# GpSimd divides the attention probabilities by their sums in place, ahead of the transposes

## The chip, the cores and the metric

One core of one Trainium2 chip runs the whole kernel. The metric is device time in microseconds (us), the median of several executions. Engines: TensorE (PE; PEld is its weight load), VectorE (DVE), ScalarE (ACT), GpSimd (POOL) and SyncE (SP), which only issues transfers.

## What is computed

One transformer block with adaptive layernorm over x of shape (8, 512, 256) in float32: latent attention with 16 heads and a causal mask, then a mixture of 16 experts (top 4, capacity 128) with a shared expert. The part that the change touches is the softmax and what follows it:

```python
scores = jnp.einsum('bqhd,bkhd->bhqk', q_full, k_full) * scale
scores = jnp.where(causal[None, None], scores, -1e30)
probs = jax.nn.softmax(scores, axis=-1)
attn = jnp.einsum('bhqk,bkhd->bqhd', probs, v)
return attn.reshape(b, s, NH * DV) @ w_o
```

The kernel applies the key and value projections on the query and output side, so that `kmat` (the latent keys, 64 columns, and the rotary part) serves as keys and values of all heads.

## The kernel before, in words

The outer loop runs over the 8 batches (512 rows each, 4 tiles of 128), the inner one over 8 pairs of heads. The order of the instructions on each engine is written out by hand, and semaphores connect the engines. `step` exists for TensorE, ScalarE and VectorE and does one pair p (g = 8b + p counts pairs); `middle` does what lies between two batches: the attention output, second layernorm, shared expert and routing of batch b, and the projection of batch b + 1. The last pair of a batch (`last`) also carries the first layernorm of the next batch, where the other pairs carry the next pair's queries.

A pair has 8 units: for each of its two heads the four query tiles from last to first, 512, 384, 256 and 128 keys wide (`UNITS`, `UW`). For each unit:

- TensorE forms the scores in PSUM (L650 to L652, three passes).
- VectorE adds the mask, takes the negated maximum and writes the shifted scores to `probs` in SBUF (`maxima`, L1231).
- ScalarE takes the exponential in place and leaves the row sums in `psums` (`exps`, L987).
- TensorE transposes `probs` in blocks of 128 x 128 to PSUM, in six groups (`GROUPS`, `turn_probs`, L671); ScalarE copies groups 0, 1, 2 and 4 to `pT` (L996), VectorE groups 3 and 5 (L1248).
- TensorE multiplies `pT` with the values in `kmat` (`values`, L692), during the next pair's step.

The sums take a way of their own. VectorE inverts the 8 sums (L1237) and widens them to 128 x 512 (`wide`, L1238); TensorE transposes that in four blocks (`spread_sums`, L681) to PSUM bank 4; ScalarE copies it to `rb` (`sums_out`, L1004); and VectorE multiplies the result of `values` by it (`values_out`, L1257).

The order on TensorE in a step is: next pair's query projection in two halves with the scores of units 3 to 7 between, `values` of the pair before, `turn_probs` groups 0 and 1, `q_turn` (L636, the next queries, which wait for VectorE's rotary steps L1210 to L1224), groups 2 and 3, groups 4 and 5, `spread_sums`, and the next pair's scores of units 0 to 2. Unit 0 of the next pair writes bank 0, where group 3 was, so it waits for VectorE's copy of group 3:

```python
pe.wait_ge(*((pT_dve, 2 * g - 1), (pT_act, 4 * g), (pT_act, 4 * g - 1))[u])
```

On VectorE the step is: maxima of units 3 and 4, then 5 to 7, the rotary steps for the next queries, `invert_sums`, `values_out`, `q_low` (L1262, which waits for ScalarE's copy of the turned queries, L982), the copies of groups 3 and 5, `q_low` again, maxima 0 to 2. In the last pair of a batch `h1_statistics` (L1178, L1181) stands behind the maximum of unit 4 and `h1_normed` (L1185) in the place of the rotary steps; TensorE then turns h1 (L762) in two parts in the place of `q_turn`, ScalarE copies each part, and the second part waits for the copy of the first.

GpSimd has its own loop over the batches: the roots for the first layernorm (`root`, L471 and L473, two operations, which wait for `var1_ready`), roots for the rms norms, `post` (roots of the second layernorm, its scale and shift, a copy of x), `counts` (the routing counts, behind `mask_ready`), `shared`, and `scatter`, 16 indirect DMAs, three to a pair, each three held until that pair's `values` are done.

## Time and profile before

| | us |
|---|---|
| median of 3 runs | 1249.4 |
| lowest, highest | 1245.29, 1251.21 |
| the profiled execution, its own time | 1254.99 |
| its span, first to last instruction | 1253.1 |
| TensorE busy | 1177.9 |
| VectorE busy | 836.0 |
| ScalarE busy | 667.2 |
| GpSimd busy | 276.5 |

Busy time is the time in which an engine has an instruction in work. TensorE's matmuls overlap one another, and their ends are modelled, so distances between starts say more than durations. The granted TensorE clock was 0.978 of full speed over the span, and 1.00 in the stretches from 570 to 740 us that are read below. Times within the trace count from the span's start.

### The profile page before, as it was taken

The numbers are of one execution on the slowest core, as the hardware profiler recorded it, in microseconds if no ns is written. First come the engines' busy times: TensorE is split into PE (matmuls) and PEld (weight loads), VectorE is DVE, ScalarE is ACT, GpSimd is POOL, SyncE is SP. The second block draws the span as 40 slices with busy tenths as digits, with TensorE's granted clock in tenths as the row PEclk, the third lists the DMA queues.
The fourth block names the chain that finished last, engine by engine and source line by source line (L and its number), as shares of the span: only waits on it lengthen the run. The fifth ranks groups of instructions, "written<-read, shape, count | busy, mean of one in ns | idle before, by whom it ended". The sixth has DMA issues, their size and how long they took to land.

```text
span 1253.1 us, 26074 instructions
## 1 busy us (share of the span) xinstructions
PE 1177.9 (94%) x7620; PEld 953.2 (76%) x7620; DVE 836.0 (67%) x2581; ACT 667.2 (53%) x1920; POOL 276.5 (22%) x332
## 2 busy tenths in 40 slices
PE   6799999999999999999999999999999999996782
PEld 3688778887888778887888778877888778873441
DVE  3677568776777667775877677766877577756221
ACT  2476626663567536763576447663667356731220
POOL 1000122211221122113212131212221122102553
PEclk9999999999999999999999999999999999997977
DMA  9410001000200001000100001000100010004752
GB/s 304 142 57 0 1 18 51 0 0 0 67 0 0 0 17 50 0 0 11 56 0 0 0 17 50 0 0 17 50 0 0 0 50 1 0 1 136 210 129 38
DMA packets 48317, 46.17 MB, mean 37 GB/s; under 512 B 10048, under 2 KB 44960, under 8 KB 48296
## 3 DMA queue, kind: packets, MB, share of 16 engines
q1 hardware_dynamic: 29096, 30.90, 8.1%
q0 software_dynamic: 7168, 6.37, 2.8%
q10 hardware_dynamic: 12032, 8.65, 2.4%
q8 instruction: 10, 0.16, 0.1%
q14 instruction: 11, 0.09, 0.0%
HBM read 35.04 MB, written 15.11 MB: 40 GB/s over the span
## 4 chain that ended last, share of the span: by engine, by line
PE 84%; DMA 5%; DVE 4%; issue 2%; ACT 2%; SPq 1%; POOL 1%; POOLq 0%; DVEq 0%; ACTq 0%
PE PS L671 11%; PE PS L692 10%; PE PS L802 8%; PE PS L650 7%; PE PS L651 6%; PE PS L652 6%; DMA out<-x_res,toku 5%; PE PS L636 4%; PE PS L810 4%; PE PS L831 3%; PE PS L623 3%; PE PS L626 2%; PE PS L627 2%; PE PS L624 2%; PE PS L625 2%; PE PS L781 2%
## 5 line engine op out<-in xcount | busy, mean ns | idle before, releaser
L987 ACT ACTIVATE probs<-probs,nmax 128x512 f32<-128x512 f32 (+3 forms) x512 | 283.0, 554 | 124.5 <-DVE nmax L1231 121.5
L1231 DVE CUSTOM_DVE_ANT_0 probs<-PS,cmask 128x512 f32<-128x512 f32 (+3 forms) x512 | 229.3, 488 | 98.6 <-PE PS L652 96.2
L540 POOL DMA_INDIRECT tab_dram<-entry,slot x112 | 110.5, 986 | 392.4 <-PE PS L692 371.1
L650 PE MATMUL PS<-kTh,qTh 128*128 128x512 f32 (+3 forms) x512 | 177.5, 347 | 1.7 <-DVE qTl L1262 1.5
L651 PE MATMUL PS<-kTl,qTh 128*128 128x512 f32 (+3 forms) x512 | 164.9, 322 | 0.0
L652 PE MATMUL PS<-kTh,qTl 128*128 128x512 f32 (+3 forms) x512 | 164.9, 322 | 0.0
L996 ACT ACTIVATE pT<-PS 128x384 f32<-128x384 f32 (+3 forms) x320 | 127.3, 462 | 70.6 <-PE PS L671 70.5
L671 PE MATMUL PS<-ident,probs 128*128 128x128 f32 x1280 | 164.8, 275 | 0.0
L692 PE MATMUL PS<-pT,kmat 128*64 128x512 f32 (+3 forms) x1024 | 151.9, 439 | 0.3 <-issue 0.3
L671 PEld LDWEIGHTS PS<-ident,probs 128*128 128x128 f32 x1280 | 141.4, 140 | 10.3 <-issue 7.4
L692 PEld LDWEIGHTS PS<-pT,kmat 128*64 128x64 f32 x1024 | 68.0, 136 | 76.0 <-issue 62.1
L802 PE MATMUL PS<-wvo,oT 128*128 128x256 f32 x512 | 116.4, 381 | 0.0
L1262 DVE TENSOR_TENSOR qTl<-PS,qTh 128x512 fp32r<-128x512 f32 x128 | 87.1, 685 | 34.0 <-ACT qTh L982 34.0
L650 PEld LDWEIGHTS PS<-kTh,qTh 128*128 128x128 f32 x512 | 96.5, 188 | 13.2 <-issue 4.6
L802 PEld LDWEIGHTS PS<-wvo,oT 128*128 128x128 f32 x512 | 95.4, 190 | 13.7 <-issue 1.4
L1248 DVE COPY pT<-PS 128x512 f32<-128x512 f32 (+2 forms) x192 | 81.5, 462 | 31.7 <-PE PS L671 31.4
L652 PEld LDWEIGHTS PS<-kTh,qTl 128*128 128x128 f32 x512 | 96.7, 189 | 5.4
L651 PEld LDWEIGHTS PS<-kTl,qTh 128*128 128x128 f32 x512 | 96.9, 189 | 4.9 <-issue 1.7
L987 ACT ACTIVATION_READ_ACCUMULATOR probs<-probs,nmax 128x1 f32 x512 | 95.7, 187 | 0.0
L1257 DVE TENSOR_TENSOR oT<-PS,th 128x512 f32 (+1 forms) x64 | 43.8, 684 | 51.0 <-PE PS L692 51.0
L623 PE MATMUL PS<-wq0h,ql0h 128*128 (+1 forms) x256 | 74.8, 292 | 2.1 <-DVE ql1s L1447 2.1
L626 PE MATMUL PS<-wq1hh,ql1s 128*128 (+1 forms) x256 | 72.4, 283 | 0.0
(242 smaller groups left out, 2084.9 us busy)
## 6 DMA issues: line engine op xcount, KB each, us to landing
x_in<-in_x SPq DMA_DIRECT2D x8, 512.0 KB, 5.9
modb<-mod_dram SPq DMA_DIRECT2D x8, 512.0 KB, 5.4
h_dram<-mod_dram SPq DMA_DIRECT2D x1, 4096.0 KB
h_dram<-h SPq DMA_DIRECT2D x8, 512.0 KB, 3.0
out<-base SPq DMA_DIRECT2D x8, 512.0 KB
pT<-in_wo SPq DMA_DIRECT2D x1, 2048.0 KB, 10.6
tab_dram<-entry,slot POOLq DMA_INDIRECT x112
oT<-in_wqnT SPq DMA_DIRECT2D x1, 1536.0 KB, 11.2
```

The costliest lines, as they stand in the source:

```text
L540: pool.indirect_dma_start(tab_dram[:, :], bass.IndirectOffsetOnAxis(ap=slot[:, j:j + 1], axis=0), entry[:, j, :], None, bounds_check=NE * ...
L623: pe.matmul(dst, ql0h[:, tok], wq0h[:, cols], start=True, stop=False)
L626: pe.matmul(dst, ql1s[:, tok], wq1hh[:, cols], start=False, stop=False)
L650: pe.matmul(PS[:, bank, 0:n], qTh[:, h, rows_q], kTh[:, 0:n], start=True, stop=False)
L651: pe.matmul(PS[:, bank, 0:n], qTh[:, h, rows_q], kTl[:, 0:n], start=False, stop=False)
L652: pe.matmul(PS[:, bank, 0:n], qTl[:, h, rows_q], kTh[:, 0:n], start=False, stop=True).then_inc(s_ps, 1)
L671: mm = pe.transpose(PS[:, bank, col:col + P], probs[:, UO[u] + j * P:UO[u] + (j + 1) * P], ident[:])
L692: mm = pe.matmul(PS[h * KL:(h + 1) * KL, OBANK, j * P:S], kmat[:, j, 0:KL], pT[:, h, j, j * P:S], start=j == 0, stop=j == NT - 1)
L802: mm = pe.matmul(PS[:, bank, 0:H], oT[:, p, bass.ts(t, P)], wvo[:, p, :], start=p == 0, stop=p == NPAIR - 1)
L987: act.activation(probs[:, UO[u]:UO[u] + UW[u]], probs[:, UO[u]:UO[u] + UW[u]], ACT.Exp, scale=-1.0, bias=nmax[:, u:u + 1], accum_out=psums ...
L996: cp = act.activation(pT[:, h, 0:i + 1, bass.ts(i, P)], PS[:, bank, col:col + UW[u]].rearrange("p (j q) -> p j q", q=P), ACT.Copy)
L1231: dve.tensor_tensor_reduce(out=probs[:, UO[u]:UO[u] + UW[u]], in0=PS[:, SBANK[u], 0:UW[u]], in1=cmask[:, S - UW[u]:S], scale=-1.0, scalar= ...
```

## The change

The probabilities are divided by their sums before they are transposed. VectorE inverts the sums in three parts (units 0 to 2 behind the maximum of unit 4, 3 and 4 behind the last maximum, 5 to 7 where the one inversion stood). GpSimd multiplies each unit of `probs` in place by its column of `prec` (`normalise`, eight operations a pair), and `turn_probs` waits for that and no longer for the exponentials. The widening copy, the four transposes, ScalarE's copy of them and the waits on it go, and `values_out` becomes a plain copy. On GpSimd the eight multiplications of each pair stand between what was there: those of the last pair of a batch at the head of the loop, with the layernorm's roots (now `roots_rows`) between parts 1 and 2; those of the first pair behind `counts`; the others each ahead of three DMAs of the scatter, which lose their wait for `values`.

```diff
-            def roots_pre(n):
+            def roots_rows(n):
 
                 wait_alone(pool, var1_ready, NT * (n + 1))
                 root(rstd[:], mv[:, :, 1], LN_EPS, eps1, rs1_ready, n)
+
+            def normalise(g, part):
+
+                lo, hi = ((0, 3), (3, 5), (5, NU))[part]
+                wait_alone(pool, prec_ready, 3 * g + part + 1)
+                for u in range(lo, hi):
+                    unit = probs[:, UO[u]:UO[u] + UW[u]]
+                    pool.tensor_scalar(unit, unit, prec[:, u:u + 1], None, ALU.mult).then_inc(norm_ready, 1)
+
+            def normalise_pair(p, b):
+
+                for part in range(3):
+                    normalise(b * NPAIR + p, part)
+
+            def normalise_last(b, more):
+
+                g = b * NPAIR + NPAIR - 1
+                normalise(g, 0)
+                normalise(g, 1)
+                if more:
+                    roots_rows(b + 1)
+                normalise(g, 2)
...
+            for p in range(NPAIR - 1):
+                normalise_pair(p, 0)
...
-            def scatter(b):
-
-                wait_alone(pool, slot_ready, b + 2)
-                for j in range(NT * TOPK):
-                    if j % 3 == 0:
-                        wait_alone(pool, o_ps, (b + 1) * NPAIR + 1 + j // 3)
-                    pool.indirect_dma_start(
-                        tab_dram[:, :], bass.IndirectOffsetOnAxis(ap=slot[:, j:j + 1], axis=0),
-                        entry[:, j, :], None, bounds_check=NE * CAP - 1, oob_is_err=False,
-                    ).then_inc(scattered, 16)
-                pool.wait_ge(scattered, (b + 1) * NT * TOPK * 16)
-                pool.sem_inc(entries_free, 1)
+            def scatter(b, j):
+
+                pool.indirect_dma_start(
+                    tab_dram[:, :], bass.IndirectOffsetOnAxis(ap=slot[:, j:j + 1], axis=0),
+                    entry[:, j, :], None, bounds_check=NE * CAP - 1, oob_is_err=False,
+                ).then_inc(scattered, 16)
 
             with pool.Fori(0, B - 1) as b:
+                normalise_last(b, True)
                 roots_pre(b + 1)
                 post(b, b + 1)
                 counts(b, False)
+                normalise_pair(0, b + 1)
                 shared(b)
-                scatter(b)
+                wait_alone(pool, slot_ready, b + 2)
+                for p in range(1, NPAIR - 1):
+                    normalise_pair(p, b + 1)
+                    for j in range(3 * (p - 1), min(3 * p, NT * TOPK)):
+                        scatter(b, j)
+                pool.wait_ge(scattered, (b + 1) * NT * TOPK * 16)
+                pool.sem_inc(entries_free, 1)
+            normalise_last(LAST, False)
...
-                    pe.wait_ge(exp_ready, g * NU + units[-1] + 1)
+                    pe.wait_ge(norm_ready, g * NU + units[-1] + 1)
...
-                    if k == 1 and not first:
-                        pe.wait_ge(rb_ready, g)
...
-            def spread_sums(g):
-
-                pe.wait_ge(wide_ready, g + 1)
-                pe.wait_ge(pT_act, 4 * g + 2)
-                for t in range(NT):
-                    mm = pe.transpose(PS[:, RBANK, bass.ts(t, P)], wide[:, bass.ts(NT - 1 - t, P)], ident[:])
-                mm.then_inc(r_ps, 1)
...
                 turn_probs(g, first, (4, 5))
-                spread_sums(g)
                 if not last:
                     scores(g + 1, False, (0, 1, 2))
...
-            def sums_out(g):
-                act.wait_ge(r_ps, g + 1)
-                act.wait_ge(oT_ready, g + 1)
-                act.activation(rb[:], PS[:, RBANK, :], ACT.Copy).then_inc(rb_ready, 1)
...
-            def invert_sums(g):
-                dve.wait_ge(exp_ready, g * NU + NU)
-                ch.step(dve.reciprocal(prec[:], psums[:]))
-                dve.tensor_copy(wide[:].rearrange("p (t h d) -> p h t d", t=NT, h=2),
-                                prec[:].rearrange("p (h t) -> p h t", h=2).unsqueeze(3).to_broadcast(
-                                    [P, 2, NT, KL])).then_inc(wide_ready, 1)
+            def invert_sums(g, lo, hi):
+                dve.wait_ge(exp_ready, g * NU + hi)
+                dve.reciprocal(prec[:, lo:hi], psums[:, lo:hi]).then_inc(prec_ready, 1)
...
                 dve.wait_ge(o_ps, g + 1)
-                dve.wait_ge(rb_ready, g + 1)
-                dve.tensor_tensor(oT[:, p, :], PS[:, OBANK, :], rb[:], ALU.mult).then_inc(oT_ready, 1)
+                dve.tensor_copy(oT[:, p, :], PS[:, OBANK, :]).then_inc(oT_ready, 1)
...
             def step(p, b, first, last, more):
                 g = b * NPAIR + p
                 maxima(g, (3, 4))
+                invert_sums(g, 0, 3)
                 if first and more:
                     gated(b - 1, 0)
                 if last and more:
                     modulation(b + 1)
                     h1_statistics(b + 1)
                 maxima(g, (5, 6, 7))
+                invert_sums(g, 3, 5)
                 if not last:
                     for part in q_rope(g + 1):
                         part()
                 elif more:
                     h1_normed(b + 1)
-                invert_sums(g)
+                invert_sums(g, 5, NU)
                 if not first:
                     values_out(p - 1, g - 1)
```

The order of the instructions shows where this lands at two places. The first is the head of GpSimd's loop over the batches, the last pair of batch b; `rstd` is the layernorm's root, `ssq` the rms roots. Before:

```order
L471 TENSOR_SCALAR rstd<-mv 128x4
L473 TENSOR_TENSOR rstd<-rstd,mhalf 128x4
L91 ISA
L471 TENSOR_SCALAR ssq<-ssq 128x8
L473 TENSOR_TENSOR ssq<-ssq,mhalf 128x8
```

and with the change:

```order
L482 TENSOR_SCALAR probs<-probs,prec 128x512
L482 TENSOR_SCALAR probs<-probs,prec 128x384
L482 TENSOR_SCALAR probs<-probs,prec 128x256
L90 ISA
L482 TENSOR_SCALAR probs<-probs,prec 128x128
L482 TENSOR_SCALAR probs<-probs,prec 128x512
L90 ISA
L467 TENSOR_SCALAR rstd<-mv 128x4
L469 TENSOR_TENSOR rstd<-rstd,mhalf 128x4
L90 ISA
L482 TENSOR_SCALAR probs<-probs,prec 128x384
L482 TENSOR_SCALAR probs<-probs,prec 128x256
```

The roots, which came first, now have five multiplications and two waits ahead of them.

The second place is VectorE in the same last pair, from the maximum of unit 6 on. Before:

```order
L1231 ISA probs,nmax<-PS,cmask 128x256
L1231 ISA nmax 128x1
L91 ISA
L1231 ISA probs,nmax<-PS,cmask 128x128
L1231 ISA nmax 128x1
L1197 REGISTER_ALU
L1185 TENSOR_SCALAR h<-x_in,mv,rstd 128x256 x4
L1237 RECIPROCAL prec<-psums 128x8
L71 REGISTER_ALU
L1238 COPY mid<-prec 128x2x4x64
```

and with the change:

```order
L1241 ISA probs,nmax<-PS,cmask 128x256
L1241 ISA nmax 128x1
L90 ISA
L1241 ISA probs,nmax<-PS,cmask 128x128
L1241 ISA nmax 128x1
L1247 RECIPROCAL prec<-psums 128x2
L1207 REGISTER_ALU
L1195 TENSOR_SCALAR h<-x_in,mv,rstd 128x256 x4
L1247 RECIPROCAL prec<-psums 128x3
```

The reciprocal of units 3 and 4 stands behind the last maximum and ahead of h1's normalisation, that of units 5 to 7 behind it, and the widening copy is gone.

## Rows read from the trace of the kernel before

**Rows 1.** The page, busy time: engine, busy us, share, instructions

```profile
PE 1177.9 (94%) x7620; PEld 953.2 (76%) x7620; DVE 836.0 (67%) x2581; ACT 667.2 (53%) x1920; POOL 276.5 (22%) x332
```

**Rows 2.** Groups by line: busy us, mean ns of one, idle before

```profile
L681 PE MATMUL PS<-ident,mid 128*128 128x128 f32 x256 | 38.4, 273 | 0.0
```

**Rows 3.** Timeline, TensorE, a steady pair: start us, us, what

```profile
625.34 0.50 PE L650 MATMUL PS<-kTh,qTh 128*128 128x512 f32 x1
...
634.01 0.98 PE L671 MATMUL PS<-ident,probs 128*128 128x128 f32 x7
634.83 1.04 PE L636 MATMUL PS<-ident,qtok 128*128 128x128 f32 x8
635.70 1.58 PE L671 MATMUL PS<-ident,probs 128*128 128x128 f32 x13
637.12 0.60 PE L681 MATMUL PS<-ident,mid 128*128 128x128 f32 x4
637.55 0.49 PE L650 MATMUL PS<-kTh,qTh 128*128 128x512 f32 x1
```

**Rows 4.** Timeline, ScalarE, the same pair; idle time ahead in brackets

```profile
634.70 0.98 ACT L996 ACTIVATE pT<-PS 128x512 f32<-128x512 f32 x2 [1.24 <-PE PS L671]
635.56 1.09 ACT L982 ACTIVATE qTh<-PS 128x512 fp32r<-128x512 f32 x2
```

**Rows 5.** Timeline, VectorE, the same pair and the copy of the pair before

```profile
624.60 1.43 DVE L1248 COPY pT<-PS 128x512 f32<-128x512 f32 x3 [0.16 <-PE PS L671]
...
632.32 0.69 DVE L1210 TENSOR_TENSOR qr<-PS,cos_sb 128x512 f32<-128x512 f32 x1
...
633.70 0.69 DVE L1224 TENSOR_TENSOR qtok<-qr 128x512 f32<-128x512 f32 x1
634.31 0.20 DVE L1237 RECIPROCAL prec<-psums 128x8 f32<-128x8 f32 x1
634.54 0.43 DVE L1238 COPY mid<-prec 128x512 f32<-128x512 f32 x1
...
636.20 0.69 DVE L1262 TENSOR_TENSOR qTl<-PS,qTh 128x512 fp32r<-128x512 f32 x1 [0.64 <-ACT qTh L982]
636.81 0.68 DVE L1248 COPY pT<-PS 128x512 f32<-128x512 f32 x1
```

**Rows 6.** Groups by line and shape, GpSimd: busy us, mean ns of one

```profile
L494 POOL TENSOR_TENSOR h<-h,modb 128x1024 f32<-128x1024 f32 x8 | 18.9, 2361 | 21.3 <-PE PS L774 21.3
L500 POOL COPY x_res<-x_in 128x1024 f32<-128x1024 f32 x7 | 7.3, 1036 | 0.0
L465 POOL CAST seat<-iota_s 128x128 f32<-128x128 int32 x1 | 0.3, 283 | 0.0
```

**Rows 7.** Timeline, last pair of a batch, three engines

```profile
693.26 0.38 DVE L1181 BATCH_NORM_AGGREGATE mv<-st 128x2 f32<-128x6 f32 x4
693.81 0.22 POOL L471 TENSOR_SCALAR rstd<-mv 128x4 f32<-128x4 f32 x1 [8.72 <-DVE mv L1181]
694.12 1.05 POOL L473 TENSOR_TENSOR rstd<-rstd,mhalf 128x4 f32<-128x4 f32 x1
694.65 0.08 DVE L1231 DVE_READ_ACCUMULATOR2_ANT nmax<- 128x1 f32 x1
695.27 1.38 DVE L1185 TENSOR_SCALAR h<-x_in,mv,rstd 128x256 f32<-128x256 f32 x4 [0.54 <-POOL rstd L473]
695.61 0.98 PE L671 MATMUL PS<-ident,probs 128*128 128x128 f32 x7
696.71 0.66 PE L762 MATMUL PS<-ident,h 128*128 128x128 f32 x4
700.20 4.57 PE L831 MATMUL PS<-wkva_sb,hT 128*128 128x320 f32 x16 [0.22 <-ACT pT L996]
```

**Rows 8.** Timeline, first pair of a batch, GpSimd and VectorE

```profile
607.87 0.23 POOL L521 TENSOR_SCALAR tid<-tid 128x4 f32<-128x4 f32 x1 [0.16 <-POOL entry L520]
608.97 0.69 DVE L1224 TENSOR_TENSOR qtok<-qr 128x512 f32<-128x512 f32 x1
```

More of the change, by code:

```diff
@@ L47 @@
 GROUPS = [((0,), 3), ((1,), 4), ((2, 3), 2), ((4,), 0), ((5,), 1), ((6, 7), 3)]
-RBANK = 4
 OBANK, QBANKS = 5, [6, 7]
@@ L51 @@
 SA, CA, GA, SB, CB, GB = range(6)
-CHAIN_PROLOGUE, CHAIN_PAIR, CHAIN_BATCH = 36, 4, 84
+CHAIN_PROLOGUE, CHAIN_PAIR, CHAIN_BATCH = 35, 3, 76
 COUNT_STEPS = NT + 2
@@ L181, in adaln_block @@
         mid = sb("mid", [P, S])
-        wide = mid
-        rb = th
         midT = sb("midT", [P, 3, S])
@@ L297, in adaln_block @@
         exp_ready = sem("exp_ready")
-        wide_ready = sem("wide_ready")
-        r_ps = sem("r_ps")
-        rb_ready = sem("rb_ready")
+        prec_ready = sem("prec_ready")
+        norm_ready = sem("norm_ready")
         pT_ps = sem("pT_ps")
@@ L473, in root, with roots_pre @@
                 pool.tensor_tensor(dst, dst, mhalf[:, 0:dst.shape[1]], ALU.pow).then_inc(ready, 1)
-            def roots_pre(n):
+            def roots_rows(n):
                 wait_alone(pool, var1_ready, NT * (n + 1))
                 root(rstd[:], mv[:, :, 1], LN_EPS, eps1, rs1_ready, n)
+            def normalise(g, part):
[14 more added lines that the diff above has]
+                normalise(g, 2)
+            def roots_pre(n):
                 wait_alone(pool, ssq_ready, 8 * (n + 1))
@@ L527, in shared @@
                 pool.tensor_tensor(base[:], tmp[:], x1[:], ALU.add).then_inc(base_ready, 1)
+            roots_rows(0)
             roots_pre(0)
@@ L1020, in step @@
                 group_out(g, 4)
-                sums_out(g)
                 if not last:
```

## The prediction, as it was made

> **What bounds the kernel now.** The page's busy row comes first: TensorE works 94% of the span [rows 1]. That says which engine a saving has to reach. It does not say that every TensorE instruction taken away is a saving, because TensorE runs ahead in order and another engine may be due at the same moment. So I went to the group of the four transposes [rows 2] and then to the timeline of one steady pair, engine by engine.
>
> The four transposes of the sums start at 637.12 and the first scores of the next pair at 637.55 [rows 3]. They hold TensorE for 0.43 us. Between the first probability transpose (634.01) and those scores lie 3.54 us.
>
> Now the same 3.54 us from the other side. The scores of unit 0 write PSUM bank 0, so they also wait for VectorE's copy of group 3 out of that bank. ScalarE's two group copies start at 634.70 and its copies of the turned queries at 635.56 [rows 4]. VectorE waits for the first of these, subtracts from 636.20, and starts its copy of group 3 at 636.81, for 0.68 us [rows 5]. That copy ends at 637.49, 0.06 us before the scores begin. In the pair before, the copy starts later (624.60 [rows 5]) and the scores start at 625.34 [rows 3]: 0.74 us after the copy's start in both pairs. So the transposes of the sums fill a gap that the copy would leave open anyway. The same distance, taken for the other pairs that have scores behind the transposes (56 in all), reads 0.73 to 0.75, but for the very first pair (0.82).
>
> The second place is the last pair of each batch, where the next batch's layernorm is threaded in. VectorE aggregates the variances (693.26), GpSimd forms the roots (693.81, 694.12), VectorE normalises h1 at 695.27, TensorE turns h1 at 696.71, and the next batch's projection starts at 700.20 [rows 7]. TensorE's turn starts right where h1 is ready (695.27 + 1.38 = 696.65). Behind it TensorE and ScalarE alternate (turn, copy, turn, copy, group copy) up to 700.20, so this stretch moves with h1.
>
> **The change part by part.** Durations are of the profiled execution: 1254.99 us, with a span of 1253.1. It stands 5.6 us above the median of 1249.4; I add the same difference to the median.
>
> Steady pairs (56 with scores behind them). Gone from TensorE: 4 transposes, 0.43 us [rows 3], 24 us over 56 pairs if all of it counted. What is late next is VectorE's copy of group 3, ready 0.06 us before TensorE's present start. ScalarE's and VectorE's steps up to it do not get shorter: ScalarE loses only the eviction that comes after its group copies, and VectorE had idle time (0.64 us ahead of 636.20 [rows 5]) in which the widening copy (0.43 us [rows 5]) was hidden. Lower bound of the saving 0, upper bound from the wait 0.06 x 56 = 3 us. I take 0, since the release of a semaphore needs part of the 0.06.
>
> The added reciprocals. Three instead of one; each takes 0.20 us (634.31 [rows 5]). The first falls in VectorE's wait for the next scores. The second stands ahead of the rotary steps, so the rotated queries come at 634.59 instead of 634.39. TensorE takes them up at 634.83 [rows 3]. The third replaces the one of before. Cost 0, cover 0.24 us; without the cover 0.2 us a pair, 11 us.
>
> GpSimd's multiplications. No row has this operation at this width. The nearest is the one-input copy of 1024 columns, 1.04 us, with the one-input cast of 128 columns at 0.28 us; the upper end is the two-input operation of 1024 columns, 2.36 us [rows 6]. I take the one-input line, since one tensor is read: 0.61 us for 512 columns, 0.50, 0.39 and 0.28 for the others, two pieces of each width make 3.6 us of a pair's 12.2 us (625.34 to 637.55 [rows 3]). Units 5 to 7 are the late ones. Their reciprocal ends at 634.79, GpSimd wakes 0.17 us later (as at 693.64 to 693.81 [rows 7]) and ends at 635.46, 635.85 and 636.13. TensorE reaches their transposes at about 636.46 and 636.8 (7 and 10 of the 13 that start at 635.70 [rows 3]). Hidden, with 0.6 us to spare. Units 3 and 4 have the second reciprocal, which takes the place of the rotary steps (632.32 [rows 5]): it ends at 632.52, GpSimd starts near 632.7 and ends near 633.6, 2 us before their transposes. The scatter, three indirect DMAs a pair, now follows unit 7 and stands ahead of nothing that TensorE wants soon: the next units' reciprocal comes some 8 us after unit 7's.
>
> First pair of a batch. GpSimd's counting ends at 608.10 [rows 8] and only then come the eight units. They end near 611.7. In the steady pair the first transpose comes 0.31 us after the addition of the rotated halves starts (634.01 against 633.70) and the last group 2.8 us after that; counted from 608.97 that is 609.3 and 612.1. Just hidden. But VectorE's addition of the rotated halves (608.97, now 609.17 [rows 8]) meets a GpSimd unit. It reads two tiles in SBUF, and no row of before has it beside a GpSimd operation that reads SBUF, so its price is bounded by 0 and by one unit's 0.39 us: I take 0.2 us x 7 = 1.4 us.
>
> The Trainium skill ("SBUF — State Buffer", section on who interferes with whom) says that a VectorE instruction with two SBUF inputs and a GpSimd instruction that reads SBUF exclude each other, the later one waiting for the whole of the earlier. By that rule this term would be 0.2 to 0.4 us a batch, by the rows alone it might be nothing. No run here shows it yet.
>
> Last pair of batches 0 to 6. This is the term that decides. The roots for the next batch are moved behind the multiplication of units 3 and 4, whose reciprocal comes after the last three maxima. Before, the roots started at 693.81, while VectorE was still at those maxima. Now:
> - last maximum ends 694.65 + 0.08 = 694.73 [rows 7], later by the first reciprocal, 0.20: 694.93
> - second reciprocal 0.20, GpSimd's wake 0.17: 695.30
> - unit 3 0.28, unit 4 0.61: 696.19
> - next wait about 0.1, then the two root steps, 1.36 (693.81 to 694.12 + 1.05 [rows 7]): 697.65
> - VectorE's wake 0.10: 697.75, against 695.27.
>
> That is 2.48 us; operations that follow without a wait overlap a little, so I take 2.4. h1, its turn, and through the alternation behind it the projection are later by it: the four transposes that stood ahead of 700.20 gave no time, since TensorE waited there for a ScalarE copy. The units 5 to 7 come after h1 (reciprocal near 699.2, done by 700.5), ahead of TensorE, which is behind the second turn of h1 by then (about 701). 7 x 2.4 = 17 us.
>
> Last batch's last pair, the expert part, the prologue: 0; values wait there for group copies.
>
> Sum: 0 + 1.4 + 17 = about +18 us: 1273 for the profiled execution, **1267** against the median.
>
> **The rivals.** First, **the transposes come back**. This is the other side. If the start of the next scores were TensorE's own work and the copy merely happened to land then, or if VectorE, free of its widening copy, pulled the copy forward, each pair would give 0.43 us: 56 x 0.43 = 24 us. With the 17 of the last pairs the net is -7 us, 1242. For it: the page's 94%, and the same 0.42 to 0.43 in nearly all pairs, which is what four transposes take. Against it: 0.74 us from the copy's start in a pair where the copy was late. It decides once pairs give back more than 0.30 us each (17 / 56). 0.08.
>
> Second, **part of it comes back**, 0.1 to 0.3 us a pair, since a chain of five steps over three engines need not be as stiff as I read it: net 0 to +12 us. 0.14, of which 0.07 lie within 0.5%.
>
> Third, **GpSimd is slow**. At 2.3 ns a column (2.36 us for 1024 [rows 6]) units 3 and 4 take 1.48 instead of 0.89 us. The last pair then costs 3.0 us, 21 in all. In a steady pair they would end at 634.2, after VectorE's addition of the halves wants to start (633.90); if the two exclude each other that addition ends at 634.9, 0.1 us after TensorE wants it, 6 us over the pairs, and the first pair of a batch is late by about 0.5 us. Together about +30, 1279. For it: GpSimd's rows hold no scaling by a column of numbers. 0.10.
>
> That the change doesn't do what it says I leave out: the order of instructions shows the four transposes and the eviction gone.
>
> **How the numbers follow.** A difference of 0.5% is 6 us, about what a measurement tells from none. The forecast (+12 to +24, the ends of the GpSimd rate and a saving of 3 us) has 0.68. The range goes from part of the transposes coming back to the slow GpSimd, 1252 to 1281; it leaves out the first rival and the far side of the others. Slower: 0.68 + 0.10 + 0.07 = 0.85. Within 0.5%: 0.07 and 0.01 of the first rival, 0.08. Faster: 0.07.
>
> **What would show it.** In a steady pair, scores start 3.5 us after the first probability transpose as before, with TensorE idle ahead of them, released by VectorE's copy; starts at 3.1 us would bring the first rival. In the last pair the roots start near 696.2 on the old scale, VectorE waits 2.5 us or more for them and TensorE as long for h1. GpSimd's 512-column units read 0.6 us; 1.2 would mean the third rival. The prediction is wrong if the last pair's stretch from first transpose to projection, 4.59 us now (695.61 to 700.20 [rows 7]), is not about 2.4 us longer.

## The result, and the profile after

The changed kernel takes **1455.25 us** (median of 4 runs, 1453.28 to 1456.41) against 1250.12 us for the kernel before on the same chip: a ratio of 1.164, 95% interval 1.1613 to 1.1667. The forecast was 1267 us, with a range up to 1281. The sign was right, and the size was missed by 188 us.

The page after, first the busy row (engine, busy us, share, instructions), then the two lines of the chain that ended last:

```profile
PE 1230.4 (85%) x7364; PEld 959.9 (66%) x7364; DVE 825.1 (57%) x2645; ACT 637.5 (44%) x1856; POOL 828.9 (57%) x844
...
PE 47%; POOL 24%; issue 17%; DVE 4%; DMA 3%; SPq 1%; POOLq 1%; ACT 1%; DVEq 1%; ACTq 0%
POOL probs L482 23%; PE PS L818 7%; PE PS L679 5%; PE PS L678 5%; PE PS L677 5%; PE PS L696 3%; PE PS L847 3%; PE PS L797 2%; DMA out<-x_res,toku 2%; PE PS L799 2%; PE PS L650 2%; PE PS L651 1%; PE PS L652 1%; PE PS L709 1%; PE PS L653 1%
```

GpSimd went from 276.5 us [rows 1] to 828.9 us, and a line that didn't exist before holds 23% of the chain. TensorE has fewer instructions (7364 instead of 7620) and reads *more* busy time, 1230.4 instead of 1177.9 us. That is a sign to look at its clock: the mean granted clock is 0.943, before it was 0.978.

The groups by line and shape give the price of the new operation (busy us, mean ns of one, idle before), and the view of waits says who stands still for it (us in total, times, longest):

```profile
L482 POOL TENSOR_SCALAR probs<-probs,prec 128x512 f32<-128x512 f32 x128 | 199.7, 1560 | 214.5 <-DVE prec L1247 214.5
L482 POOL TENSOR_SCALAR probs<-probs,prec 128x384 f32<-128x384 f32 x128 | 158.7, 1240 | 12.2 <-DVE prec L1247 12.2
L482 POOL TENSOR_SCALAR probs<-probs,prec 128x256 f32<-128x256 f32 x128 | 118.0, 922 | 0.0
L482 POOL TENSOR_SCALAR probs<-probs,prec 128x128 f32<-128x128 f32 x128 | 82.7, 646 | 0.0
```

```profile
PE PS L696 <- POOL probs L482: 122.2, 187, 1.0
PE PS L778 <- DVE h L1195: 28.8, 7, 4.1
```

512 columns take 1.56 us where the forecast took 0.61. The four widths lie close to a line of (1560 - 646) / 384 = 2.38 ns a column above a fixed 0.34 us. Two units of each width make 8.7 us a pair, not 3.6.

**A steady pair.** The timeline of one, TensorE, GpSimd and VectorE (start us, us, what, idle ahead in brackets):

```profile
757.78 0.99 PE L696 MATMUL PS<-ident,probs 128*128 128x128 f32 x7
...
760.37 0.65 PE L696 MATMUL PS<-ident,probs 128*128 128x128 f32 x4 [0.41 <-POOL probs L482]
761.59 0.54 PE L696 MATMUL PS<-ident,probs 128*128 128x128 f32 x3 [0.57 <-POOL probs L482]
763.07 0.54 PE L696 MATMUL PS<-ident,probs 128*128 128x128 f32 x3 [0.94 <-POOL probs L482]
763.37 0.48 PE L677 MATMUL PS<-kTh,qTh 128*128 128x512 f32 x1
```

```profile
754.30 8.64 POOL L482 TENSOR_SCALAR probs<-probs,prec 128x512 f32<-128x512 f32 x8 [1.85 <-DVE prec L1247]
763.11 1.02 POOL L560 DMA_INDIRECT tab_dram<-entry,slot  x1 [0.17 <-issue]
```

```profile
753.96 0.17 DVE L1247 RECIPROCAL prec<-psums 128x3 f32<-128x3 f32 x1
...
767.57 0.69 DVE L1241 CUSTOM_DVE_ANT_0 probs<-PS,cmask 128x512 f32<-128x512 f32 x1 [0.44 <-PE PS L679]
...
768.18 0.17 DVE L1247 RECIPROCAL prec<-psums 128x3 f32<-128x3 f32 x1
```

These rows form a closed ring. The first reciprocal starts at 753.96, GpSimd at 754.30, and it works on all eight units without a gap until 762.94. TensorE starts the last group 0.13 us later (763.07), the next pair's scores 0.30 us after that (763.37), and 4.81 us later VectorE has the maxima up to unit 4 behind it and starts the next first reciprocal (768.18). So the ring is 0.34 + 0.13 + 0.30 + 4.81 = 5.58 us plus GpSimd's 8.64: 14.22 us. The pair before took 12.2 to 12.5 us. The transposes and next scores now are 5.59 us apart (757.78 to 763.37), against 3.54 [rows 3].

Behind all of this lies a condition that the prediction lacked. The 48 steady pairs before take 12.35 us in the mean, and the ring stays hidden in that only while GpSimd needs less than about 6.8 us for its eight units.

**One batch, stretch by stretch.** Each row runs from one start of `values` to the next (us, TensorE's busy us, its granted clock, DMA share, GB/s): after, a steady pair, another, the last pair, and the stretch with `middle` and the first pair's multiplications; then the same kinds before.

```profile
414.53:428.75 14.22, 12.31 (x89) 1.00 0.01 0
428.75:444.52 15.77, 13.87 (x89) 0.89 0.00 0
...
488.98:505.90 16.92, 12.77 (x62) 0.80 0.00 0
505.90:563.94 58.04, 53.90 (x295) 0.97 0.11 32
```

```profile
356.04:368.32 12.28, 12.28 (x94) 1.00 0.01 0
...
417.67:429.05 11.38, 10.96 (x66) 1.00 0.00 0
429.05:481.25 52.20, 51.65 (x299) 1.00 0.11 34
```

Adding all such stretches up splits the 200.3 us between the two spans:

| stretch, by starts of `values` | before | after | difference |
|---|---|---|---|
| 48 steady pairs | 592.7 | 704.7 | +112.0 |
| 7 last pairs | 79.8 | 116.0 | +36.2 |
| 7 middles | 365.4 | 408.7 | +43.3 |
| the rest of the span | 215.2 | 224.0 | +8.8 |

**The clock.** In 12 of the 48 steady pairs the mean granted clock reads 0.89, and they take 1.5 us longer, as 15.77 instead of 14.22 us above. The 0.89 is a mean over the pair: the clock is at 1.00 except in one piece, which reads 0.50 (436.9 to 440.2 us in the pair from 428.75), the lower of the two levels (1.2 of 2.4 GHz). In the kernel before it reads 1.00 in all 48. Inside the pair from 428.75:

```profile
428.75:434.00 5.25, 4.85 (x38) 1.00 0.00 0
434.00:439.50 5.50, 4.00 (x18) 0.76 0.01 0
```

TensorE had just waited for GpSimd three times (0.40, 0.57 and 0.94 us), and then the clock falls: the next scores of 384 columns take 0.53 us instead of the 0.34 that they take at full clock. Around the end of the first pair of a batch the granted clock is 0.50 for 6 us (717 to 723 us). In the steady pairs the lowered clock makes 12 x 1.5 = 18 of the 112 us.

**The last pair.** GpSimd and TensorE:

```profile
487.70 5.81 POOL L482 TENSOR_SCALAR probs<-probs,prec 128x512 f32<-128x512 f32 x5 [6.07 <-DVE prec L1247]
493.50 0.22 POOL L467 TENSOR_SCALAR rstd<-mv 128x4 f32<-128x4 f32 x1
```

```profile
491.29 0.98 PE L696 MATMUL PS<-ident,probs 128*128 128x128 f32 x7
496.39 1.12 PE L778 MATMUL PS<-ident,h 128*128 128x128 f32 x4 [4.12 <-DVE h L1195]
...
501.16 3.19 PE L847 MATMUL PS<-wkva_sb,hT 128*128 128x320 f32 x10
```

The roots started 1.80 us before the first transpose [rows 7] and now start 2.21 us after it. From the first transpose to the projection it takes 9.87 us instead of 4.59. Part of this is the clock, which reads 0.68 over these 9.87 us. All seven last pairs have a lowered clock here, 0.66 to 0.84, and take 9.1 to 9.9 us.

**The first pair.** The counts end as before, and the eight multiplications stand behind them:

```profile
708.89 8.52 POOL L482 TENSOR_SCALAR probs<-probs,prec 128x512 f32<-128x512 f32 x8
```

```profile
717.54 0.90 PE L696 MATMUL PS<-ident,probs 128*128 128x128 f32 x3 [0.94 <-POOL probs L482]
```

Before, the next pair's scores started 4.6 us after the last step of the counts (612.70 against 608.10, see [rows 8] for the counts). Now the eight units alone take 8.5 us behind the counts, and the scores start at 718.09, 9.2 us after 708.89. That is 4.6 of the 6.2 us that a middle has grown by; behind it comes the stretch at the lower clock.

### The profile page after: what moved, and what is told of

The parts are those of the page before. It is cut to its first block, busy times and chain, and to the rows that moved or that the text cites. A ratio compares the mean times of both kernels' runs of the same rounds, so it can differ in the third digit from the quotient of the medians.

```text
span 1453.4 us, 26009 instructions
## 1 busy us (share of the span) xinstructions
PE 1230.4 (85%) x7364; PEld 959.9 (66%) x7364; DVE 825.1 (57%) x2645; ACT 637.5 (44%) x1856; POOL 828.9 (57%) x844
## 4 chain that ended last, share of the span: by engine, by line
PE 47%; POOL 24%; issue 17%; DVE 4%; DMA 3%; SPq 1%; POOLq 1%; ACT 1%; DVEq 1%; ACTq 0%
POOL probs L482 23%; PE PS L818 7%; PE PS L679 5%; PE PS L678 5%; PE PS L677 5%; PE PS L696 3%; PE PS L847 3%; PE PS L797 2%; DMA out<-x_res,toku 2%; PE PS L799 2%; PE PS L650 2%; PE PS L651 1%; PE PS L652 1%; PE PS L709 1%; PE PS L653 1%
## 5 line engine op out<-in xcount | busy, mean ns | idle before, releaser
L482 POOL TENSOR_SCALAR probs<-probs,prec 128x512 f32<-128x512 f32 (+3 forms) x512 | 551.5, 1092 | 226.8 <-DVE prec L1247 226.8
L696 PE MATMUL PS<-ident,probs 128*128 128x128 f32 x1280 | 214.5, 293 | 123.2 <-POOL probs L482 122.2
L1241 DVE CUSTOM_DVE_ANT_0 probs<-PS,cmask 128x512 f32<-128x512 f32 (+3 forms) x512 | 233.2, 488 | 118.7 <-PE PS L679 116.8
L677 PE MATMUL PS<-kTh,qTh 128*128 128x512 f32 (+3 forms) x512 | 182.9, 357 | 1.5 <-DVE qTl L1268 1.5
L679 PE MATMUL PS<-kTh,qTl 128*128 128x512 f32 (+3 forms) x512 | 175.8, 343 | 0.0
L678 PE MATMUL PS<-kTl,qTh 128*128 128x512 f32 (+3 forms) x512 | 175.8, 343 | 0.0
L677 PEld LDWEIGHTS PS<-kTh,qTh 128*128 128x128 f32 x512 | 104.2, 203 | 7.9 <-issue 3.4
L679 PEld LDWEIGHTS PS<-kTh,qTl 128*128 128x128 f32 x512 | 105.1, 205 | 6.1
L678 PEld LDWEIGHTS PS<-kTl,qTh 128*128 128x128 f32 x512 | 104.4, 204 | 6.2 <-issue 1.7
L651 PE MATMUL PS<-wq0l,ql0h 128*128 (+1 forms) x256 | 73.9, 289 | 0.0
```

The costliest lines, as they stand in the source:

```text
L482: pool.tensor_scalar(unit, unit, prec[:, u:u + 1], None, ALU.mult).then_inc(norm_ready, 1)
L677: pe.matmul(PS[:, bank, 0:n], qTh[:, h, rows_q], kTh[:, 0:n], start=True, stop=False)
L678: pe.matmul(PS[:, bank, 0:n], qTh[:, h, rows_q], kTl[:, 0:n], start=False, stop=False)
L679: pe.matmul(PS[:, bank, 0:n], qTl[:, h, rows_q], kTh[:, 0:n], start=False, stop=True).then_inc(s_ps, 1)
L696: mm = pe.transpose(PS[:, bank, col:col + P], probs[:, UO[u] + j * P:UO[u] + (j + 1) * P], ident[:])
L1241: dve.tensor_tensor_reduce(out=probs[:, UO[u]:UO[u] + UW[u]], in0=PS[:, SBANK[u], 0:UW[u]], in1=cmask[:, S - UW[u]:S], scale=-1.0, scalar= ...
```

## The experiments

Two theories stood at the start. **Price**: the kernel's order and waits are as the prediction read them, and what is wrong is GpSimd's price alone. **Structure**: the waits themselves (three reciprocals, units in this order behind them, the roots and counts) bind, whatever the operation costs. The first four runs keep every instruction's place and change only what GpSimd does with a unit. Each ratio below is to the kernel before on the same chip; that kernel's median was 1257.39 us on the chip of these four, and 1250 to 1253 us on the others.

### GpSimd copies instead of multiplying

```diff
-                    pool.tensor_scalar(unit, unit, prec[:, u:u + 1], None, ALU.mult).then_inc(norm_ready, 1)
+                    pool.tensor_copy(unit, unit).then_inc(norm_ready, 1)
```

> GpSimd copies each unit of probs in place instead of multiplying it; the division is left out, all else is the change. Theory A (the column of numbers as the second operand makes GpSimd slow): the copy follows the rows of before, 512 columns near 0.6 us where the multiplication takes 1.56, the eight of a pair near 3.6 us instead of 8.6, and the time falls to about 1267 us, the forecast. Theory B (in-place work on probs beside the other engines' reads of it is slow, whatever the operation): the copy takes 1.5 us too and the time stays at 1455.

Measured: 1269.67 us, ratio 1.0088 (1.0069 to 1.0108). Groups by shape, and the first pair's timeline:

```profile
L482 POOL COPY probs<-probs 128x512 f32<-128x512 f32 x128 | 78.4, 613 | 259.3 <-DVE prec L1247 259.3
L482 POOL COPY probs<-probs 128x128 f32<-128x128 f32 x128 | 40.7, 318 | 42.6 <-DVE prec L1247 42.5
```

```profile
480.09 3.68 POOL L482 COPY probs<-probs 128x512 f32<-128x512 f32 x8
```

and VectorE's addition of the rotated halves, by its line (shortest, median and longest in ns, first and last start):

```profile
L1234 DVE TENSOR_TENSOR qtok<-qr x64: 691/693/905, 48.7 to 1114.1; 128x512 f32<-128x512 f32 x64
```

This kernel is the one the prediction describes: 0.61 us for 512 columns, 3.7 us for eight units, steady pairs of 12.20 us, and last pairs of 13.4 us where the clock stays at 1.00 (14.7 where it reads 0.88). It is slower by 11 us where the forecast had 18. So the one-input line was right for a copy, and a multiplication doesn't lie on it. At full clock the way from the first transpose to the projection is 6.6 us, 2.0 more than the 4.6 of before. The addition takes 0.69 us in the 57 pairs where no copy runs beside it, and 0.90 us in the seven first pairs of a batch where one does.

### A constant instead of the column of reciprocals

```diff
-                    pool.tensor_scalar(unit, unit, prec[:, u:u + 1], None, ALU.mult).then_inc(norm_ready, 1)
+                    pool.tensor_scalar(unit, unit, 1.0, None, ALU.mult).then_inc(norm_ready, 1)
```

> The same with a multiplication by the constant 1.0; the division is left out. Theory A (the column operand is the cost): as fast as the copy, 0.6 us for 512 columns, about 1267 us. Rival (GpSimd's one-input arithmetic is slow with any operand, only the copy is fast): 1.5 us for 512 columns, 1455 us.

Measured: 1410.89 us in one run. The operation does as the rival said. The time is 44 us below the 1455 that it gave, and GpSimd's eight units are 0.77 us shorter a pair (7.87 against 8.64).

```profile
L482 POOL TENSOR_SCALAR probs<-probs 128x512 f32<-128x512 f32 x128 | 190.5, 1489 | 210.0 <-DVE prec L1247 209.4
```

The column operand costs 0.07 us of the 1.56; the arithmetic costs the rest. The ring is tested here too. A steady pair on GpSimd:

```profile
599.18 7.87 POOL L482 TENSOR_SCALAR probs<-probs 128x512 f32<-128x512 f32 x8 [2.19 <-DVE prec L1247]
```

With 5.58 + 7.87 the ring gives 13.45 us, and the steady pairs take 13.82. GpSimd's 0.77 us less are there, and the rest of the ring is 0.36 us longer: between the scores and the next reciprocal it is 5.17 instead of 4.81 us, since VectorE waits 1.32 instead of 0.53 us ahead of the maximum of unit 3. What holds it there I didn't find.

### The same product as an operation on two tensors

```diff
-                    pool.tensor_scalar(unit, unit, prec[:, u:u + 1], None, ALU.mult).then_inc(norm_ready, 1)
+                    pool.tensor_tensor(unit, unit, prec[:, u:u + 1].to_broadcast([P, UW[u]]), ALU.mult).then_inc(norm_ready, 1)
```

> The multiplication as a two-tensor operation with the column of reciprocals spread over the unit; it computes the same as the change. If the two-tensor rate of before holds (2.36 us for 1024 columns, 0.22 for 16), 512 columns take 1.27 us, the eight of a pair 7.0 instead of 8.6 us, and with GpSimd setting the pair's length the time falls by some 1.6 us a pair, to about 1350 to 1370 us. If a spread column is read no faster than the column operand: 1.56 us and 1455.

Measured: 1297.58 us in one run, with the whole computation in it: less than the 1350 to 1370 expected, since the operation is faster than the 1.27 us taken from before.

```profile
L482 POOL TENSOR_TENSOR probs<-probs,prec 128x512 f32<-128x512 f32 x128 | 135.9, 1061 | 210.0 <-DVE prec L1247 210.0
L1234 DVE TENSOR_TENSOR qtok<-qr 128x512 f32<-128x512 f32 x64 | 66.8, 1044 | 2.2
```

The form with two inputs is the faster one: 1.06 us instead of 1.56 for 512 columns, 5.8 us for eight units. That is below the 6.8 us of the ring, and the steady pairs are back at 12.3 us: four fifths of the loss go by changing the form of one instruction. The second row shows a new cost, though: VectorE's addition of the rotated halves, 0.69 us before [rows 5], takes 1.04 us in the mean (1.09 in the 56 that have a multiplication beside them, 0.69 in the other 8).

### One column of each unit

```diff
-                    unit = probs[:, UO[u]:UO[u] + UW[u]]
+                    unit = probs[:, UO[u]:UO[u] + 1]
```

> Each multiplication is cut to one column of its unit (the other columns are not divided); waits and order are those of the change. It asks what is left of the loss without GpSimd's time. My reading of the rows: steady pairs end as before (12.2 to 12.5 us, the four transposes give nothing, TensorE waits for VectorE's copy of group 3), the last pair of seven batches is longer by about 2 us, the time is 1258 to 1265 us. Rival (the transposes do count once GpSimd is out of the way): pairs of 11.8 us and 1240 us or less.

Measured: 1265.34 us, ratio 1.0054 (1.0036 to 1.0073).

```profile
L482 POOL TENSOR_SCALAR probs<-probs,prec 128x1 f32<-128x1 f32 x512 | 139.6, 289 | 443.7 <-DVE prec L1247 443.0
```

All waits of the change are in it, and 2.3 of GpSimd's 8.7 us a pair. Steady pairs take 12.20 and middles 52.2 us, no more than before; the last pairs 13.2 to 14.3 instead of 11.4, the longer ones with a clock of 0.88. So the waits cost nothing but in the last pair, and the theory of structure holds for that place alone. How much it is there reads differently by trace and by time: the seven last pairs add 16.2 us (96.0 against 79.8), the ratio says 7 us. The 48 steady pairs are 5.2 us shorter here than in the one trace of before (587.5 against 592.7), which belongs to an execution 5.6 us above its median; the other 4 us stay open.

### The kernel before without the way of the sums

```diff
                 turn_probs(g, first, (4, 5))
-                spread_sums(g)
...
-                sums_out(g)
...
-                dve.wait_ge(rb_ready, g + 1)
-                dve.tensor_tensor(oT[:, p, :], PS[:, OBANK, :], rb[:], ALU.mult).then_inc(oT_ready, 1)
+                dve.tensor_copy(oT[:, p, :], PS[:, OBANK, :]).then_inc(oT_ready, 1)
```

> The kernel before without the transposes of the sums, ScalarE's copy of them and the division in values_out (a plain copy); nothing is divided. VectorE's widening copy stays. My reading (VectorE's copy of group 3 sets the start of the next scores): pairs of 12.2 us at least, as the shortest of before, so 0 to 8 us faster, scores still 0.73 to 0.75 us after that copy's start, and TensorE idle ahead of them. Rival (the four transposes are on the path): 0.43 us a pair, 24 us faster, pairs of 11.8 us.

Measured: 1251.15 us, ratio 1.000 (0.9986 to 1.0014). TensorE and VectorE in a steady pair:

```profile
637.77 0.50 PE L650 MATMUL PS<-kTh,qTh 128*128 128x512 f32 x1 [0.26 <-DVE pT L1244]
```

```profile
637.04 1.21 DVE L1244 COPY pT<-PS 128x512 f32<-128x512 f32 x3
```

256 transposes and 64 evictions fewer, and nothing gained. Where the transposes stood, TensorE now waits, and the row names who it waits for: VectorE's copy of group 3. From the copy's start to the scores it is 0.73 us, the distance that the prediction had read from before. (In the two profiled executions the 48 steady pairs differ by 5.7 us, 0.1 us a pair; the timed runs don't show it, and the traced execution of before lay 5.6 us above its median.)

### Roots ahead of the multiplication of units 3 and 4

```diff
                 normalise(g, 0)
-                normalise(g, 1)
                 if more:
                     roots_rows(b + 1)
+                normalise(g, 1)
```

> The change with the next batch's layernorm roots ahead of the multiplication of units 3 and 4 instead of behind it; same computation. If the roots' place costs what I read (units 3 and 4 stand in their way, here 0.65 + 1.56 us), seven last pairs get shorter by 2 us or a little more: about 15 us faster than the change, 1440 to 1450 on a chip where before is 1250 to 1257. Rival (in the last pair GpSimd's multiplications bound the end anyway, so the order is indifferent): within 4 us of the change.

Measured: 1437.01 us, ratio 1.1502 (1.1472 to 1.1533), 18 us less than the change. The last pairs fall from 16.1 to 16.9 us to 13.67 in six of seven. Its TensorE row, to be read against the wait of 4.12 us above:

```profile
487.95 0.65 PE L778 MATMUL PS<-ident,h 128*128 128x128 f32 x4 [2.36 <-DVE h L1195]
```

### The same with one column of each unit

```diff
 (one column of each unit as above, and)
-                normalise(g, 1)
                 if more:
                     roots_rows(b + 1)
+                normalise(g, 1)
```

> Multiplications cut to one column (as in a4) and the roots ahead of units 3 and 4 (as in b2). If the 2 to 3 us by which a4's last pairs are longer are the place of the roots, they go: last pairs near 11.5 us, and about 5 us faster than the kernel before. If they stay at 13 to 14 us, it is the reciprocals or the number of GpSimd's instructions.

Measured: 1251.96 us, ratio 1.001 (0.9996 to 1.0024); last pairs 11.47 us. The pairs are as expected, the time isn't: it is level with the kernel before, not 5 us faster. With this one exchange the ratio falls from 1.0054 to 1.001, and the seven last pairs from 96.0 to 80.3 us: what the change's structure cost was the place of the roots.

### The first reciprocal ahead of the maxima of units 3 and 4

```diff
-                maxima(g, (3, 4))
                 invert_sums(g, 0, 3)
+                maxima(g, (3, 4))
```

> The change with the reciprocal of units 0 to 2 ahead of the maxima of units 3 and 4; same computation. In the change a pair is a ring: first reciprocal, GpSimd 8.6 us without a gap, last transposes, the next scores and maxima up to the next first reciprocal. If that ring sets the pair, taking the reciprocal from behind two maxima (0.9 to 1.1 us) shortens steady pairs from 14.2 to 13.2 to 13.4 us and the kernel by 30 to 55 us. Rival (TensorE or ScalarE sets the pair): no change.

Measured: 1398.44 us, ratio 1.1192 (1.1162 to 1.1221), 57 us less than the change. Steady pairs take 13.65 instead of 14.23 us, VectorE and GpSimd:

```profile
421.59 0.18 DVE L1247 RECIPROCAL prec<-psums 128x3 f32<-128x3 f32 x1 [1.15 <-ACT probs L1003]
```

```profile
421.94 8.79 POOL L482 TENSOR_SCALAR probs<-probs,prec 128x512 f32<-128x512 f32 x8 [1.12 <-DVE prec L1247]
```

The scores of this ring start at 417.51, so the reciprocal comes 4.08 us behind them instead of 4.81. Of these 0.73 us the pair keeps 0.58; GpSimd's eight units take 8.79 instead of 8.64 us. It is less than the 0.9 to 1.1 us of the two maxima, since the reciprocal now waits for ScalarE's exponential of unit 2 (1.15 us). An engine at 67% and then 57% busy is on the path because of *where* its 0.17 us operation stands. In its 48 steady pairs the clock is never below 1.00, so the 18 us of the lowered clock come back as well: 28 + 18 of the 50 us by which these 48 are shorter.

### The order of two groups exchanged, without the way of the sums

If VectorE's late copy of bank 0 is what holds the next scores, filling that bank one group earlier must shorten the pair. By its new place in the order the group is also copied out by ScalarE and no longer by VectorE; the two are not separated here.

```diff
-GROUPS = [((0,), 3), ((1,), 4), ((2, 3), 2), ((4,), 0), ((5,), 1), ((6, 7), 3)]
+GROUPS = [((0,), 3), ((1,), 4), ((4,), 0), ((2, 3), 2), ((5,), 1), ((6, 7), 3)]
...
-                        pe.wait_ge(*((pT_dve, 2 * g - 1), (pT_act, 4 * g), (pT_act, 4 * g - 1))[u])
+                        pe.wait_ge(*((pT_act, 4 * g - 1), (pT_act, 4 * g), (pT_dve, 2 * g - 1))[u])
...
-                        pe.wait_ge(max_ready, g * NU + k + 4)
+                        pe.wait_ge(max_ready, g * NU + (7, 7, 8)[k - 2])
```

> b1 (no transposes of the sums, nothing divided) with groups 2 and 3 exchanged: the transposes of unit 4, whose bank the next scores need first, come ahead of those of units 2 and 3, and ScalarE copies them out, VectorE the others. If b1's gap ahead of the next scores is the road to the copy out of bank 0, the road gets shorter by about 0.35 us (ScalarE's copy ends near 3.1 us after the first transpose instead of 3.48), pairs go from 12.2 to about 11.85 us and the kernel is 15 to 22 us faster than before. Rival (the pair is held elsewhere, the copy only happens to land then): within 5 us of b1, which was level with the kernel before.

Measured: 1235.26 us, ratio 0.9855 (0.9838 to 0.9871). It leaves the division out, so it is no finished kernel, but a lower bound for what the removal could bring.

```profile
624.34 0.98 PE L669 MATMUL PS<-ident,probs 128*128 128x128 f32 x7
...
626.03 1.58 PE L669 MATMUL PS<-ident,probs 128*128 128x128 f32 x13
627.53 0.50 PE L650 MATMUL PS<-kTh,qTh 128*128 128x512 f32 x1
```

From the first transpose to the next scores it is 3.19 us, and no wait stands ahead of the scores.

### The exchange alone, on the kernel before

The same edit to the kernel before, with the sums' transposes in place.

> The kernel before with groups 2 and 3 exchanged (bank 0 is filled and copied out one group earlier) and nothing else: the sums are still widened, transposed and copied. It completes the square of with and without the sums' transposes, in the old and in the new order of the groups. Theory (in the old order VectorE's late copy of bank 0 hides the four transposes; in the new order that cover is gone): the transposes now cost 0.2 to 0.43 us a pair of the 56, 11 to 24 us on top of the 0.9855 of the exchange without them; ratio 0.994 to 1.005, steady pairs 12.1 to 12.4 us. Rival (the pairs of the exchange without them, 11.85 to 12.08 us, were already held by another engine's chain, which hides the transposes as well): steady pairs stay at 11.85 to 12.1 us, ratio 0.985 to 0.990, a kernel faster than both.

Measured: 1241.6 us, ratio 0.9928 (0.9913 to 0.9942), the whole computation in it: **0.7% below the kernel before**, clear of the interval, and below the changed one.

```profile
618.57 0.98 PE L671 MATMUL PS<-ident,probs 128*128 128x128 f32 x7
...
621.68 0.60 PE L681 MATMUL PS<-ident,mid 128*128 128x128 f32 x4
622.04 0.48 PE L650 MATMUL PS<-kTh,qTh 128*128 128x512 f32 x1
```

Here it is 3.47 us. The square of four now reads:

| ratio to the kernel before | old order | groups exchanged |
|---|---|---|
| with the sums' transposes | 1 | 0.9928 |
| without them | 1.000 | 0.9855 |

The transposes cost nothing that a measurement tells (0.14% either way) where the copy of bank 0 comes late, and about 0.7%, 9 us, where it doesn't. The expected ratio (0.994 to 1.005) was just too high and the rival's (0.985 to 0.990) just too low: the transposes do cost, but less than the 0.28 us between 3.19 and 3.47, since the 48 steady pairs are 12.15 us in the mean with them and 12.05 without. What takes back the difference within the pair I didn't follow.

### The division on GpSimd, made as cheap as the findings allow

The change with the form on two tensors, the roots behind the multiplication of unit 1, the first pair's multiplications ahead of the counts, and the last reciprocal ahead of the last rotary step.

```diff
-                    pool.tensor_scalar(unit, unit, prec[:, u:u + 1], None, ALU.mult).then_inc(norm_ready, 1)
+                    pool.tensor_tensor(unit, unit, prec[:, u:u + 1].to_broadcast([P, UW[u]]), ALU.mult).then_inc(norm_ready, 1)
...
-                normalise(g, 0)
-                normalise(g, 1)
+                wait_alone(pool, prec_ready, 3 * g + 1)
+                multiply(0, 2)
                 if more:
                     roots_rows(b + 1)
+                multiply(2, 3)
+                normalise(g, 1)
...
-                counts(b, False)
                 normalise_pair(0, b + 1)
+                counts(b, False)
```

> A mended form of the change, which divides all of probs: the multiplication as a two-tensor operation (5.8 instead of 8.6 us a pair), the roots behind units 0 and 1, the first pair's multiplications ahead of the counts, the last reciprocal ahead of the last rotary step. If the terms found so far are all there is, steady pairs are 12.2 us, the last pair 11.5 to 12, the stretch between the batches 52.2 to 52.6, and the time is level with the kernel before, -3 to +6 us.

Measured: 1276.1 us, ratio 1.017 (1.0148 to 1.0192), 21 us slower where -3 to +6 was expected. The terms found so far are not all there is. The steady pairs take 12.41 us in the mean, the last pairs 12.48 and the middles 53.6; with one column of each unit and the roots ahead they took 12.23, 11.47 and 52.2.

With the exchange of the groups on top of it:

> v0 with groups 2 and 3 exchanged as in c1; divides all of probs. If both readings hold, pairs are 11.85 to 12.0 us and the kernel beats the one before by 8 to 20 us. If GpSimd's units 6 and 7 now come after TensorE wants them (they are ready about 2.8 us after the first transpose, wanted at 2.7), half of it goes: 5 to 10 us. Rival (GpSimd's 5.8 us hold the pair at 12.2): level with v0.

Measured: 1257.65 us, ratio 1.0035 (1.002 to 1.0051). That is within half a per cent of before, and behind the exchange alone; 8 to 20 us faster than before was expected. The steady pairs are as good as without any division (12.06 us in the mean against 12.05). The last pairs (12.1 us against 11.2 of the exchange without the sums) and the middles (53.7 against 52.0) aren't. GpSimd, VectorE and TensorE in the first pair:

```profile
759.26 5.92 POOL L485 TENSOR_TENSOR probs<-probs,prec 128x512 f32<-128x512 f32 x8 [3.16 <-DVE prec L1252]
```

```profile
762.10 1.46 DVE L1239 TENSOR_TENSOR qtok<-qr 128x512 f32<-128x512 f32 x1
```

```profile
763.71 1.06 PE L668 MATMUL PS<-ident,qtok 128*128 128x128 f32 x8 [0.86 <-DVE qtok L1239]
```

VectorE's addition lies within GpSimd's work and takes 1.46 instead of 0.69 us, and TensorE waits 0.86 us for it. That is one visible part of what is left; the counts, late now behind the multiplications, are another that I name without having tested it.

## Why the prediction was right in sign and wrong in size

- **Failed: the price of GpSimd's multiplications.** "I take the one-input line, since one tensor is read: 0.61 us for 512 columns" is the step. Measured: 1.56 us, and 8.6 instead of 3.6 us a pair. The copy in the same place read 0.61 us and gave 1.0088, so this one step holds nearly all of the missing 188 us. Copy and arithmetic are different kinds. The nearest row for arithmetic was the two-input operation [rows 6], which I took for the upper end; the measured 1.56 us lies above its 2.3 ns x 512 = 1.18 us too.
- **Failed with it: the third rival's consequences.** Its rate, 2.3 ns a column, was close to the 2.38 measured, yet it came to +30 us. It drew a line through zero, which makes 2560 columns 5.9 us; the fixed 0.34 us of eight instructions adds 2.7 us and takes the sum past the 6.8 us at which the ring binds. A fixed part could be read beforehand: the same kind of instruction on 4 columns takes 0.22 us [rows 7], which with 5.9 us gives an estimate of 7.7 us. And it asked only whether units 3 and 4 are late for VectorE. It never closed the path from the first reciprocal over all eight units to the next pair's first reciprocal, which is what sets the pair.
- **Failed: the range.** Its upper end was the third rival's time, so it took over that rival's error whole. 8.6 us of a pair of 12.3 us, with 5.6 us of other engines' work in the same ring, had nowhere to hide.
- **Right: the steady pair's saving is 0.** Taking the sums' way out gave a ratio of 1.000, with the wait on VectorE's copy that the prediction named. Exchanging two groups uncovered what had been hidden. The rival of transposes that come back is ruled out for this order of groups.
- **Right in mechanism, mis-sized: the last pair.** The forecast was 2.4 us each, 17 in all. With the copy, the last pairs are longer by 2.0 us at full clock, and by 19.8 in all, the five at a clock of 0.88 included. At the real price it is 36 us in all (with the lowered clock in it), and moving the roots gives back 18: the way from the first transpose to the projection, named as the sign of being wrong, is 5.3 us longer and not 2.4. With one column a unit the place of the roots alone is 15.7 us by the last pairs of the two traces, 5.5 by the ratios.
- **Failed: the first pair.** Forecast 0.2 us a batch, from VectorE's addition meeting a GpSimd unit, with GpSimd's eight units "just hidden" at 3.6 us. Measured 6.2 us a batch; 4.6 of them are the length of GpSimd's work at its real price, the rest is not taken apart. For the operation that was priced, the copy, the term was right: the addition takes 0.90 instead of 0.69 us in all seven first pairs, and a middle grows by 0.1 us. Beside the scaling of the change itself (757.54 in the steady pair above, inside GpSimd's 8.64 us) it reads 0.69 us as before in 51 of 56 pairs, and 0.75 to 0.85 in five. The Trainium skill ("SBUF — State Buffer", section on who interferes with whom) has two such instructions exclude each other. With GpSimd's copy and with its form on two tensors (1.09 us in the mean) this case's traces agree in direction; the 0.21 us beside the copy is less than the 0.36 us that the earlier copy still had to run. With its scaling they do not agree.
- **Not foreseen: the clock.** No term of the sum had TensorE running slower. 12 steady pairs lost 1.5 us each by it, and the last pair shown above, at 0.80, lost by it too.
- **Failed, small: the last batch's last pair.** Forecast 0; the distance between its two starts of `values` grew from 5.5 to 8.4 us, and with the copy it stayed at 5.5. So this too is the price.

## What to carry to other kernels

Price an added operation by a row of the same kind of work (a copy says nothing of arithmetic), with its fixed part times the number of instructions, and where no row has it, carry the upper bound through the whole loop before calling it unlikely. For every engine that is put *into* a loop, close the ring: start at the first thing that releases it, go round to the same point of the next turn, and write down the time at which it binds; here 6.8 us, which one form of the instruction meets (5.8) and the other misses (8.6). And removing work from the busiest engine gains nothing where another engine's copy ends at the same moment; moving that copy one place forward, onto another engine, gained 9 us, where taking the sums' way out gained none.

## What the runs showed of the hardware

- GpSimd on float32, 128 partitions, 512 columns: copy 0.61 us, product of two tensors (one of them a broadcast column) 1.06 us, scaling by a column or a constant 1.56 and 1.49 us. Per column 0.77, 1.73 and 2.38 ns; the form that reads more is the faster one.
- The smallest such scaling, of one column, takes 0.29 us.
- TensorE's granted clock fell to 0.50 for a piece of 12 of 48 steady pairs (mean over the pair 0.89), and stayed at 1.00 over the other 36, 31 of which have the same waits of 0.4, 0.6 and 0.9 us. With waits of 0.56 and 0.94 us (the reciprocal moved ahead) it fell in none of 48. With the constant it fell in 5 of 48, and in each of these five the first wait was 0.91 us; in the 43 others, with about 0.24, 0.48 and 0.77 us, it didn't.
- VectorE's operation with two SBUF inputs (0.69 us alone) kept its 0.69 us beside GpSimd's scaling by a constant in 56 of 56 cases and by a column in 51 of 56. It took 0.90 us beside GpSimd's copy in 7 of 7, where the GpSimd copy of 128 columns behind it took 0.75 instead of 0.29 us, and 0.78 to 1.56 us beside GpSimd's operation on two tensors.
